# A frequency's channels side by side, padded input spectra, one tile shape for the filter turns, and a new order in the token norm

## The reference

```
x = x + L0_conv(_ln_c(x), ...)              # linear attention, 4 heads of 32
t = _to_tokens(x)                           # (32, 256, 32)
t = t + L0_ffn(_ln_t(t), sigma, phi, M_u, M_phi_plus, M_phi_minus, ...)
```

```
U_plus  = irfft(rfft(phi) * rfft(u))[:, :sl]
U_minus = irfft(rfft(phi) * rfft(u * sgn))[:, :sl] * sgn
out = einsum('btkd,k,kde->bte', U_plus, s, Mpp) + einsum(..., U_minus, s, Mpm) + taps
```

## Time and profile before

| | |
|---|---|
| median of 3 runs | 416.87 us |
| lowest, highest | 412.98, 418.19 us |
| the profiled execution | 420.25 us, of which the span of the trace is 418.4 us |
| mean granted TensorE clock | 0.963 |
| busy share TensorE, DVE, ScalarE, GpSimd | 92%, 54%, 45%, 8% |

### The profile page before, as it was taken

How to read it: one execution, slowest core, us unless ns; L and a number is a source line. 1 busy time by engine, 2 the same in 40 slices (tenths; PEclk the granted TensorE clock), 3 DMA queues, 4 the chain that set the end, 5 groups by cost and what they waited for, 6 DMA issues and landing times.

```text
span 418.4 us, 8639 instructions
## 1 busy us (share of the span) xinstructions
PE 382.9 (92%) x3638; PEld 249.3 (60%) x3638; DVE 227.2 (54%) x453; ACT 186.7 (45%) x402; POOL 32.9 (8%) x39
## 2 busy tenths in 40 slices
PE   7948999999999899999888989799998999999891
PEld 2525665656556699546654539636745764674691
DVE  3669767768847302121565764673337147434885
ACT  2858677676574400031292445560247115124361
POOL 0038211212210000001000000000000000000000
PEclk9998999999999999999999999989999579999996
DMA  9970000004910000200000000000000000000004
GB/s 226 166 194 3 2 2 3 2 2 98 218 41 2 3 2 2 52 1 2 0 2 2 2 0 2 4 0 2 0 2 0 2 0 2 1 2 2 0 2 104
DMA packets 7528, 11.97 MB, mean 29 GB/s; under 512 B 3758, under 2 KB 6462, under 8 KB 6974
## 3 DMA queue, kind: packets, MB, share of 16 engines
q1 hardware_dynamic: 5822, 10.32, 11.4%
q10 hardware_dynamic: 1664, 1.05, 0.9%
HBM read 6.65 MB, written 1.05 MB: 18 GB/s over the span
## 4 chain that ended last, share of the span: by engine, by line
PE 72%; DVE 10%; ACT 7%; DMA 5%; issue 3%; SPq 2%; DVEq 0%; ACTq 0%
PE bank L642 31%; PE bank L844 7%; PE bank L265 6%; PE bank L1076 6%; DMA arena<-in_w_spec 5%; PE bank L259 4%; PE bank L1006 4%; PE bank L1017 3%; ACT lnv L364 1%; PE bank L1132 1%; PE bank L738 1%; PE bank L750 1%; SPq L536 1%; ACT rs L369 1%; DVE arena L1745 1%
## 5 line engine op out<-in xcount | busy, mean ns | idle before, releaser
L358 ACT ACTIVATE sq<-bank 128x512 f32<-128x512 f32 x34 | 20.0, 592 | 68.1 <-PE bank L259 53.8
L642 PE MATMUL bank<-sb_consts 128*128 128x512 f32 (+1 forms) x104 | 48.3, 578 | 1.6 <-ACT arena L1441 1.6
L642 PE MATMUL bank<-xn,sb_w_attn 128*128 128x512 f32 x64 | 35.4, 635 | 7.6 <-ACT attn_scratch L1210 6.6
L265 PE MATMUL bank<-sq,sb_consts 128*128 128x512 f32 x68 | 35.7, 610 | 0.6 <-ACT sq L358 0.3
L364 ACT ACTIVATE lnv<-bank 128x512 f32<-128x512 f32 x34 | 20.3, 597 | 34.6 <-PE bank L265 34.5
L844 PE MATMUL bank<-xn,arena 128*128 128x512 f32 (+15 forms) x112 | 31.1, 428 | 0.0
L1076 PEld LDWEIGHTS bank<-arena,sb_w_late 128*128 128x128 f32 x180 | 23.0, 191 | 11.2 <-DVE arena L1804 8.0
L1076 PE MATMUL bank<-arena,sb_w_late 128*128 128x128 f32 x180 | 27.2, 287 | 1.7 <-DVE arena L1804 1.3
L642 PEld LDWEIGHTS bank<-sb_consts 128*128 128x128 f32 x104 | 18.7, 199 | 15.8 <-issue 13.7
L1017 PE MATMUL bank<-arena,sb_w_late 128*128 128x128 f32 x144 | 27.9, 276 | 0.0
L1006 PE MATMUL bank<-arena,sb_consts 128*128 128x128 f32 x144 | 27.7, 276 | 0.1
(11 more groups left out here) (207 smaller groups left out, 652.7 us busy)
## 6 DMA issues: line engine op xcount, KB each, us to landing
arena<-arena SPq DMA_DIRECT2D x4, 512.0 KB, 8.8
arena<-in_w_spec SPq DMA_DIRECT2D x2, 720.0 KB
sb_w_late<-in_w_late SPq DMA_DIRECT2D x1, 1100.5 KB, 23.7
arena<-arena SPq DMA_DIRECT2D x4, 256.0 KB, 4.1
arena<-fourier SPq DMA_DIRECT2D x1, 768.0 KB, 21.5
sb_w_attn<-in_w_attn SPq DMA_DIRECT2D x1, 641.0 KB, 9.1
xR<-in_x SPq DMA_DIRECT2D x4, 128.0 KB, 4.0
xR<-in_x ACTq DMA_DIRECT2D x4, 128.0 KB, 4.1
```

Of the source, the lines that this page charges most:

```text
L265: pe.matmul(bank[:, var_bank(i), :], mean32, sq[:, i % 2, :], start=True, stop=True)\
L358: act.activation(sq[:, i % 2, :], bank[:, centre_bank(i), :], ACT.Square).then_inc(S("ln_squared"), 1)
L642: return mm(ps, lhsT, rhs, start=True, stop=True)
```

## The change

It has five parts. (1) `w_f` is stored with the 32 channels of one spectral number side by side; ScalarE's copy in line 1241 now writes its elements 32 apart. (2) `x_f` has four unused elements behind each batch's 128, so that batches lie 132 elements (528 bytes) apart; `y_f` moves to the place of x_tok. (3) A filter turn first does the eight spectral matmuls and then makes the lags by eight matmuls of 64 rows and 32 weight columns in place of two with 128 columns. (4) Segment 3 stands ahead of the 128 matmuls of the spectral stage and waits for the first half of xn alone; the wait for its second half moves to segment 1. (5) In the token norm DVE puts `tok_sum(0)` and `tok_sum(1)` between the last `attn_apply`s and keeps its first two spectra later (`keep_spectrum(1)` behind all applies), ScalarE issues `tok_square` one part ahead of `tok_rstd`, and TensorE's two `keep_busy` are gone.

```diff
-        w_f = arena[:, 0:N_W].rearrange("p (e n) -> p e n", e=C)
-        w_fr = arena[:, 0:N_W].rearrange("p (e r f) -> p f r e", e=C, r=2)
+        w_f = arena[:, 0:N_W].rearrange("p (n e) -> p e n", e=C)
+        w_fr = arena[:, 0:N_W].rearrange("p (r f e) -> p f r e", e=C, r=2)
...
-        x_f = attn_scratch[:, 1024:1024 + B * FREQ].rearrange("p (g n) -> p g n", g=G)
-        x_fb = attn_scratch[:, 1024:1024 + B * FREQ].rearrange("p (b f) -> p f b", b=B)
-        y_f = attn_scratch[:, 5120:5120 + 2 * C * B].rearrange("p (r e b) -> p r e b", r=2, b=B)
+        x_fp = attn_scratch[:, 1024:1024 + B * (FREQ + 4)].rearrange("p (b f) -> p b f", b=B)[:, :, 0:FREQ]
+        x_f = x_fp.rearrange("p (g q) f -> p g q f", q=NQ)
+        x_fb = x_fp.rearrange("p b f -> p f b")
+        y_f = attn_scratch[:, 7168:7168 + 2 * C * B].rearrange("p (r e b) -> p r e b", r=2, b=B)
...
-                for half in range(2):
-                    full(bank[:, 4 + half, 2 * FREQ:2 * FREQ + HT],
-                         wm_raw.rearrange("p f (d e) -> p (f d) e", e=C)[two[half], :, C // 2 * half + m],
-                         phi_cols[two[half], 0:HT])
+                wm = wm_raw.rearrange("p f (d e) -> p f d e", e=C)
                 for k in range(4):
                     for half in range(2):
-                        last = full(bank[C * k:C * k + C, 4 + half, 0:2 * FREQ],
-                                    wm_raw.rearrange("p f (d e) -> p f d e", e=C)[two[half], 0, :, C // 2 * half + m],
-                                    phi_f[two[half], 2 * FREQ * k:2 * FREQ * k + 2 * FREQ])
+                        full(bank[C * k:C * k + C, 4 + half, 0:2 * FREQ], wm[two[half], 0, :, C // 2 * half + m],
+                             phi_f[two[half], 2 * FREQ * k:2 * FREQ * k + 2 * FREQ])
+                for n in range(FRACS):
+                    for half in range(2):
+                        last = full(bank[C * n:C * n + C, 4 + half, 2 * FREQ:2 * FREQ + HT],
+                                    wm[two[half], n, :, C // 2 * half + m], phi_cols[two[half], 0:HT])
...
             token_chunk(1)
-            keep_busy(BUSY[2], 7)
             token_chunk(2)
-            keep_busy(BUSY[2], 7)
             token_chunk(3)
...
+            pe.wait_ge(S("ln_applied"), ln_at(2) + 1)
+            segment(3, 0, 8, 6)
...
-            pe.wait_ge(S("ln_applied"), ln_at(3))
-            segment(3, 0, 8, 6)
             segment(2, 8, 16, 6)
...
+            pe.wait_ge(S("ln_applied"), ln_at(3))
             segment(1, 16, 32, 7, beside)
...
             ln_rstd(act, CH + 3)
+            tok_square(1)
             tok_rstd(0)
-            for j in range(1, CH):
-                tok_square(j)
-                tok_rstd(j)
+            tok_square(2)
+            tok_rstd(1)
+            tok_square(3)
+            tok_rstd(2)
+            tok_rstd(3)
...
-            ln_dve(dve, 1, attn_apply)
...
             for j in range(CH):
-                tok_sum(j)
+                dve.wait_ge(S("ln_rstd"), CH + j + 1)
+                attn_apply(j, CH + j)
+                if j >= 2:
+                    tok_sum(j - 2)
+            for j in range(CH):
+                if j < 2:
+                    tok_sum(j + 2)
                 tok_apply(j)
-                if j == 2:
-                    keep_spectrum(1)
+            keep_spectrum(1)
             keep_spectrum(3)
```

More of the change, by code:

```diff
@@ L1292, in keep_spectrum @@
                 act.wait_ge(S("x_f_ps"), g + 1)
-                act.activation(x_f[:, g, :], bank[:, DFT_BANKS[g], :], ACT.Copy).then_inc(S("x_f_act"), 1)
+                act.activation(x_f[:, g, :, :], bank[:, DFT_BANKS[g], :].rearrange("p (q f) -> p q f", q=NQ), ACT.Copy).then_inc(S("x_f_act"), 1)
             ln_square(act, CH + 2)
@@ L1579, in keep_spectrum @@
                 dve.wait_ge(S("x_f_ps"), g + 1)
-                dve.tensor_copy(x_f[:, g, :], bank[:, DFT_BANKS[g], :]).then_inc(S("x_f_dve"), 1)
+                dve.tensor_copy(x_f[:, g, :, :], bank[:, DFT_BANKS[g], :].rearrange("p (q f) -> p q f", q=NQ)).then_inc(S("x_f_dve"), 1)
             def rows_apply(a):
```

## The result

The changed kernel took 403.25 us (median of 4 runs, 402.22 to 410.67), the kernel before 417.53 us on the same chip. The ratio is 0.967, 95% interval 0.958 to 0.976. Some executions of the same kernel take over 1.5% longer at a lower granted clock; all ratios leave them out, the medians don't. The forecast was 405.7 us, a ratio of 0.973, with a range of 401 to 411. The profiled execution took 402.22 us, its span is 400.3 us, 18.1 less than the 418.4 of before.

The account below looks back on a forecast made before the run. TensorE was taken as the bound. Gains of 7.3 (spectral matmuls), 2.0 (filter turns), 0.9 (token norm) and 1.0 (segment 3) sum to 11.2 us: 409.05 from the profiled 420.25, ratio 0.973, 405.7 on the median; range 401 to 411.

Parts of the forecast that it names:

- What bounds the kernel: Whole kernel, first half above all: TensorE, busy 92% of the span, sets the time if no other engine takes over.
- Spectral matmuls: Spectral stage, 128 matmuls: from 92.6 to 35 ns each, 11.85 to 4.5 us, gain 7.3 us (3.7 to 8.7).
- The cacheline rule: Spectral stage: by the skill's 16-byte-line rule the padding would do nothing; the forecast sided with the trace, 92.6 against 58 ns.
- Weight loads: Spectral stage: strided weight loads stay hidden; not hidden at all, 56 ns a matmul and 7.2 us.
- The rival at 408.9: Spectral stage: weight loads or the left-over 35 ns set the pace, 7.2 to 8.2 us, total gain 8.0; chance 0.15.
- Filter turns and ScalarE: Attention loop: turns fall from 1.31 to 1.0 us, ScalarE's strided copy closes the loop at 6.1 us; gain 2.0 us.
- Token norm: Before the first transform: tok_sum(0) fits ahead of attn_apply(3), so the first transform starts sooner; gain 0.9 us (0 to 1.6).
- Segment 3 first: Ahead of the spectral stage: segment 3 fills TensorE's 1.2 us wait for DVE's last spectrum; gain 1.0 us (0.5 to 1.2).
- The clock rival: Token norm: TensorE's clock falls where the kept-busy matmuls were, 1.7 us lost, total gain 9.5, time 407.4; chance 0.15.
- The slower one: Attention loop: ScalarE's strided eviction costs far more, deciding from 1.8 us; at 2.0 us the time is 420; chance 0.03.
- nothing comes of the turns: Attention loop: lags cost what spectra do and ScalarE's eviction is the bound, -0.2 for 2.0, total 9.0; chance 0.12.
- the strides don't set the spectral stage's pace: Spectral stage: the layout change does nothing, 11.85 us stays, total gain 3.9, time 413.0; chance 0.05.

## Why the prediction was right, step by step

**What bounds the kernel** held for the kernel before: TensorE's time there was the kernel's, and the first stretches lost 12.6 us where 11.2 were forecast. The 1.4 between them is 1.65 in the turns, 0.33 in the token norm and 0.08 at segment 3, less 0.66 in the spectral stage. In the changed kernel TensorE is the bound no longer in two places: it waits 2.3 us for ScalarE in the attention loop, as forecast, and 1.6 us for DVE in the token norm.

**Spectral matmuls: right in size, with the split wrong.** 35 ns a matmul was forecast and 35 was measured. But "29 are the dense work, 29 the stride as such, and 35 are left for the long distances" put 35 ns where the runs show 29 for the moving operand's 1,024 bytes and 16 for the weights' 512, each alone, and 45 if they add. With the channel step padded 63 ns remain; less the 35 of the dense and padded stage that is 28 for the plain stride, or 12 if the weights' 16 come on top of it (no run had both steps padded in the old layout). The total was right since the change removes all three.

**The cacheline rule.** The Trainium skill (SBUF — State Buffer, "Door 1: The DMA port swizzle", the box on cachelines) has every access that crosses to a new 16-byte line pay, and says nothing of how far away that line is. I read it so that the padding would do nothing, and set it against the trace. The padding alone was worth 2.06 us, so the trace disagrees with that reading, as forecast. The box also wants two hits a line for full speed. Where ScalarE writes, the runs agree with that: two elements in a line took the copy of 512 from 1,119 to 618 ns.

**Weight loads** were hidden: 35 ns a matmul, not 56. The rival at 408.9 fell. The Trainium skill (TensorE: Matmul & The Clock Gate, "The mechanism", where its list of what overlaps stands) has weight loads overlap running matmuls only where the row groups differ. By it I had worked out 7.2 us for the stage; the trace, with 4.5, disagrees. What I didn't foresee is the stall of 0.66 us. It is the difference between the forecast gain of 7.3 and the measured 6.6. (Segment 2 and 3 took 0.12 more, the work in the matmuls 0.1 less than forecast.) The loads last 148 ns, where 160 was forecast.

**Filter turns and ScalarE: the mechanism right, the size small by 1.65 us.** TensorE does wait for line 1242 ahead of the second turn, and line 1242 lasts 1,119 ns against 1,088 forecast. Two terms of the loop were off. One is "a turn is then 1.0 us": it is 0.87, as in my fastest bound. The other is "2.96 us without a pause, now 3.42". ScalarE's own timeline of the changed kernel, from the eviction of the second turn to that of the next unit's first:

```profile
87.90 0.60 ACT L1240 ACTIVATE arena<-bank 128x256 f32<-128x256 f32 x1 [0.64 <-PE bank L643]
88.31 1.10 ACT L1242 ACTIVATE arena<-bank 128x512 f32<-128x512 f32 x1
89.20 0.63 ACT L1226 ACTIVATE attn_scratch<-attn_scratch 128x512 f32<-128x512 f32 x1
...
91.14 0.63 ACT L1240 ACTIVATE arena<-bank 128x256 f32<-128x256 f32 x1
```

The stretch is 87.90 to 91.14 = 3.24 us. The next instruction starts 0.89 us behind the start of the dear copy (88.31 to 89.20), where it stood 0.52 behind the cheap one's before (91.44 to 91.96): the record grew by 0.49 us, but ScalarE's list only by 0.37, where I had added 0.46. That is half of the 0.18 by which the stretch is short of 3.42; the other half I can't place. So the loop closes at 5.86 and not at 6.1. The third part of the miss is "0.3 a unit, eight units": in units with the attention's output TensorE has some 0.9 us more to do, so ScalarE is not the bound there. They went from 7.32 to 6.47 us, a full gain of two turns, and only the unit behind them, in which ScalarE catches up, gained nothing (6.42 to 6.40). I had looked at one unit and multiplied by eight.

**Token norm: the size near by luck, the reason false.** 0.9 was forecast and 1.23 measured. My step was "in the new order tok_sum(0) fits ahead of attn_apply(3)". The old order without the kept-busy matmuls does as well, so the order isn't the cause. The rows of before already said so: DVE began tok_apply(0) at 128.64 and was done at 129.3, while the first transform began at 130.82. TensorE was late, not DVE, and its queue was full of work that nobody read.

**Segment 3 first** took the 1.2 us wait away and brought 1.08 (forecast 1.0), by the view of TensorE's waits, where the row has no successor. The transposes of y_f had 5.87 us of segment 2 as cover.

**The clock rival fell.** With the kept-busy matmuls gone the granted clock was 1.00 from 114 to 126 us and from 126 to 184, though TensorE was busy for only 10.46 of the first 12. What moved the clock lies behind the triangle, in stretches that the change doesn't touch, and both lengths of that tail occurred with the changed kernel itself.

**The other rivals.** The slower one needed line 1241 at 1.8 us; at 1.12 it wasn't near. That nothing comes of the turns (407.9) fell with their gain of 3.65 us, and that the strides don't set the spectral stage's pace (413.0) with its fall from 11.85 to 4.44 us of work.

## What to carry to other kernels

When a layout change makes one engine's reads dense, cost the other engine's writes in the same row and look for a loop order that puts two elements into each line: here that gave back 3.0 of the turns' 6.7 us. Here distances of exactly 512 or 1,024 bytes cost TensorE more than distances 16 bytes longer, so four unused elements are the first thing to try, before any rearrangement. When a bundle of edits gives the forecast gain, take it apart all the same: the new order in the token norm had no part in it, and one look at who is late, the engine that waits or the one that keeps itself busy, would have told so.

## What the runs showed that was not expected

- The distances of 1,024 and 512 bytes against 1,040 and 528: 29 ns of 92.6 in the moving operand, 16 in the weights, 7 in the weights behind a dense moving operand.
- ScalarE's price for writing with a stride is 0.9 to 1.0 ns an element by the records (1,119 against 618 ns for 512, 618 against 391 for 256), of which the next instruction in its list feels three quarters (0.37 of 0.49 us), and it vanishes with two elements a line.
- Short matmuls outrun something. A dense stage of 512 records in 4.5 us stands still once, for 0.5 to 1.3 us, without a releaser; slower stages, and the same stage with 2.8 us of longer matmuls in its middle, don't. It stands behind the 1,981st matmul record of TensorE's list, or the 1,725th, 256 earlier, whatever the code before it. That fits instructions which arrive in portions and too slowly for this stage. The cause is argued, not shown: no run changed the supply of instructions alone, and the two packets of instructions (0.03 MB) that were moved between 140 and 150 us were moved in the kernel before as well.
- In the same code, 100 to 120 us behind the triangle's first matmul, the granted clock was 0.64 or 0.65 in three profiles, with tails of 201.3 to 201.6 us, 0.83 or 0.84 in three, with 196.8 to 197.3, and 0.91 in seven, with 195.4 to 196.1. In the 20 us ahead of it TensorE was equally busy (19.55 us) at 1.00 in all thirteen. Why it differs stays open; no experiment was made on it.
